# Causal attention: weighting in one block of 512 columns, six slots of probabilities, and 512 columns of zeros added to the sums behind each block

## What is computed

```
xn = layernorm(x)
q, k, v = xn @ Wq.T + bq, xn @ Wk.T + bk, xn @ Wv.T + bv      # 16 heads of 16
p = softmax(q k^T / 4, causal: k_pos <= q_pos)                # per head, 2048 x 2048
s = (p v) @ Wo.T + bo
g = silu(two layers of windowed attention and a gated feed-forward net on xn)
out = x + s * g
```

## Time and profile before

| | us |
|---|---|
| median of 3 runs | 5207.88 |
| lowest, highest | 5165.24, 5208.1 |
| profiled execution | 5235.67 |
| its span | 5233.7 |
| `attend` in it, from the first weighing to the last | 284.6 to 2184.8 |

### The profile page before, as it was taken

The page is one execution under the profiler, slowest core; times in us unless marked ns, Lnnn a source line. Parts: engine busy times, 40 slices in busy tenths (PEclk is TensorE's granted clock), DMA queues, the critical chain, the costliest instruction groups (busy, mean ns, idle before and its releaser), DMA issues. The chain is left out here.

```text
span 5233.7 us, 99917 instructions
## 1 busy us (share of the span) xinstructions
PE 4816.1 (92%) x35808; PEld 3106.5 (59%) x35808; DVE 3696.0 (71%) x7557; ACT 3021.4 (58%) x6873; POOL 1338.9 (26%) x1844
## 2 busy tenths in 40 slices
PE   8599999999999999679999999997699999999986
PEld 7333333343433333267777777775477777777766
DVE  7477776776777777377777777773677777777746
ACT  3156666666666666445666666563366665656642
POOL 3111111111111111143333333330333333333300
PEclk9689888887979798789999999998799999999998
DMA  8623322222222232100000000000100000000007
GB/s 308 180 33 44 48 39 34 35 34 34 35 34 34 34 41 28 65 5 13 14 13 13 13 13 13 13 13 34 33 13 13 13 14 13 17 13 13 13 5 264
DMA packets 175716, 214.72 MB, mean 41 GB/s; under 512 B 75836, under 2 KB 126996, under 8 KB 169108
## 3 DMA queue, kind: packets, MB, share of 16 engines
q1 hardware_dynamic: 175252, 208.56, 17.5%
HBM read 124.05 MB, written 83.89 MB: 40 GB/s over the span
## 5 line engine op out<-in xcount | busy, mean ns | idle before, releaser
L595 ACT ACTIVATE a_pt<-a_ring 128x512 f32<-128x512 f32 (+3 forms) x2560 | 1209.9, 534 | 640.0 <-PE a_ring L678 623.2
L630 DVE TENSOR_REDUCE a_mx<-a_ring 128x2 f32<-128x1024 f32 (+3 forms) x1120 | 1180.2, 1068 | 463.8 <-PE a_ring L691 275.3
L720 PE MATMUL a_ot<-a_pt,a_vt 128*32 128x256 f32 (+2 forms) x8704 | 790.6, 438 | 4.4 <-issue 3.8
L691 PE MATMUL a_ring<-a_ks,a_qs 48*128 48x512 f32 (+3 forms) x2560 | 575.3, 445 | 134.4 <-DMA a_v_in<-v_d 51.4
L678 PE MATMUL a_ring<-a_qs,a_ks 49*128 49x512 f32 (+3 forms) x2560 | 637.6, 497 | 47.9 <-DMA a_qs<-a_ntb 19.2
L970 POOL TENSOR_TENSOR l_rn<-l_ssm,l_half 128x8 f32<-128x8 f32 x256 | 431.8, 1687 | 951.1 <-DVE l_ssm L1252 951.1
L678 PEld LDWEIGHTS a_ring<-a_qs,a_ks 49*128 49x128 f32 x2560 | 263.6, 201 | 558.5 <-issue 196.8
L572 POOL TENSOR_TENSOR a_gate<-a_gate 128x1 f32<-128x1 f32 x512 | 98.8, 193 | 1659.9 <-ACT a_pt L595 1655.1
L1071 ACT ACTIVATE l_pr<-l_pr,l_negm 128x256 f32<-128x256 f32 (+1 forms) x1024 | 500.7, 493 | 6.5 <-DVE l_negm L1304 6.1
L977 POOL TENSOR_TENSOR l_work<-l_work,l_rot 128x512 f32<-128x512 f32 x256 | 357.0, 1396 | 396.2 <-DVE l_work L1260 396.2
L1079 ACT ACTIVATE l_pts<-l_banks 128x512 f32<-128x512 f32 (+1 forms) x512 | 296.9, 580 | 271.7 <-PE l_banks L1581 210.0
(11 more groups left out here) (173 smaller groups left out, 9254.8 us busy)
## 6 DMA issues: line engine op xcount, KB each, us to landing
qk_d<-p_parts SPq DMA_DIRECT2D x16, 2048.0 KB, 10.1
a_qs<-qk_d SPq DMA_DIRECT2D x96, 256.0 KB, 8.9
a_ks<-qk_d SPq DMA_DIRECT2D x96, 256.0 KB, 18.9
x_d<-l_dx SPq DMA_DIRECT2D x32, 512.0 KB, 2.8
l_xt<-x_d SPq DMA_DIRECT2D x24, 513.0 KB, 3.9
p_x_in<-x SPq DMA_DIRECT2D x16, 512.0 KB, 8.6
x_d<-p_xt SPq DMA_DIRECT2D x16, 512.0 KB, 4.8
v_d<-p_vt SPq DMA_DIRECT2D x16, 512.0 KB, 10.4
```

The source lines that it names most:

```text
L595: act.activation(pt[:, s % NPT, j, q0:CHUNK], bank("step", k, f)[:, q0:CHUNK], ACT.Exp).then_inc(exp_done.sem, 1)
L630: r = dve.tensor_reduce(mx[:, pr, :, t, kc], ring[:, a:b + 1, 0:w], AX.X, ALU.max)
L691: mm = pe.matmul(bank("unit", n, f)[:, 0:w], qs[rows, v, pr, q0:q0 + P], ks[rows, v, pr, kc * CHUNK:kc * CHUNK + w], start=True, stop=kc < c)
L720: mm = pe.matmul(ot[j * VW:(j + 1) * VW, a:b], vt[:, v, kt, j], pt[:, s % NPT, j, a:b], start=kt == 0, stop=kt == TPC * (c + 1) - 1)
```

## The change

Each step is weighed as one block, in its second slot, over all its columns (512, on the diagonal 512, 384, 256 and 128), three steps behind instead of two (LAG = 3). `pt` gets six slots. Behind the block of every step but the last of a chunk, four more matmuls follow, one for each head: bfloat16 zeros, 512 columns, added to the same bank, so that the sums stay what they are. The step is counted as weighed (`pv_done`) when these are through. Two tiles of zeros are set by DVE at the start.

```diff
-        NPT = 4
-        LAG = 2
+        NPT = 6
+        LAG = 3
...
+        rest_w = sb("rest_w", [P, VW], BF16)
+        rest_x = sb("rest_x", [P, CHUNK], BF16)
...
+            dve.memset(rest_w[:, :], 0.0)
+            dve.memset(rest_x[:, :], 0.0)
             dve.memset(ones[:, :], 1.0).then_inc(ones_set, 1)
...
                     q0 = first_column(c, kt)
-                    halves = [(max(q0, a), a + CHUNK // 2) for a in (0, CHUNK // 2)]
-                    now = halves[piece:piece + 1] if kt else [(0, CHUNK)] if piece else []
-                    if s == 0 and piece:
+                    if not piece:
+                        return
+                    if s == 0:
                         pe.wait_ge(v_ready.sem, v_ready.at(G))
-                    if kt == 0 and piece:
+                    if kt == 0:
                         pe.wait_ge(os_ready.sem, os_ready.at(G, c))
-                    if now and kt >= TPC * c:
+                    if kt >= TPC * c:
                         pe.wait_ge(masked.sem, masked.at(G, 2 * kt + 2))
-                    elif now:
+                    else:
                         pe.wait_ge(exp_done.sem, exp_done.at(G, GH * (s + 1)))
-                    for a, b in now:
-                        for j in range(GH):
-                            if a < b:
-                                mm = pe.matmul(ot[j * VW:(j + 1) * VW, a:b], vt[:, v, kt, j],
-                                               pt[:, s % NPT, j, a:b],
-                                               start=kt == 0, stop=kt == TPC * (c + 1) - 1)
-                    if piece:
-                        mm.then_inc(pv_done.sem, 1)
+                    for j in range(GH):
+                        mm = pe.matmul(ot[j * VW:(j + 1) * VW, q0:CHUNK], vt[:, v, kt, j],
+                                       pt[:, s % NPT, j, q0:CHUNK],
+                                       start=kt == 0, stop=kt == TPC * (c + 1) - 1)
+                    if kt < TPC * (c + 1) - 1:
+                        for a in range(0, 512, CHUNK):
+                            for j in range(GH):
+                                mm = pe.matmul(ot[j * VW:(j + 1) * VW, 0:min(CHUNK, 512 - a)], rest_w[:, :],
+                                               rest_x[:, 0:min(CHUNK, 512 - a)], start=False, stop=False)
+                    mm.then_inc(pv_done.sem, 1)
```

## The result

The changed kernel takes **5286.42 us** (median of 4 runs, 5279.85 to 5307.62), the kernel before 5196.47 beside it (4 runs, 5165.24 to 5208.1): 1.0174 times as long, 95% interval 1.0137 to 1.0211. The forecast was 5270, slower than before. The profiled execution went from 5235.67 to 5284.91 us, +49 where the sum said +40.

What follows compares the result with a forecast made beforehand. Bound: a 31.5 us DMA chain from load to slot 24, then PE, with low clock costing 7.2 us a period. Terms 2.7 + 5.5 - 5.8 = +2.4 over 14 periods, +6 at the ends: 5276, taken as 5270 us; range 5170 to 5340.

Steps and rivals of the forecast that it cites:

- Part A: From a load's first DMA to slot 24: a chain of DMAs, 31.5 us, not shrunk by the change.
- The later load: Load waits for the last weighing, moved from slot 3 to slot 5: +2.7 us a period (bounds 2.2 to 3.2).
- Block, zeros and wait: Slots 24 to 79 on PE, merged blocks, added zeros and newly exposed waits together: +5.5 us a period (1.0 to 9.5).
- My sign for it: In the changed profile, the zeros row should stand 0.24 us before the following scores.
- dear zeros: Rival: each block of zeros on PE costs 0.355 us, not 0.24, 42 us more in all: 5312 us; chance 0.10.
- The wait itself: Second unit of a full step waits 0.2 to 0.4 us for the first exponential on ACT; step takes 2.91 us.
- The clock: PE's low clock behind slot 24 shrinks to 5 us, its cost from 7.2 to 1.4: -5.8 us a period.
- The sum: All terms of a period: 2.7 + 5.5 - 5.8 = +2.4 us for each of 14 periods, +34.
- The ends: First and last group, outside the periods: zeros and waits cost about 12 us, better clock returns about 6, +6.
- the clock did not pay for all: Denies the rival that zeros keep PE's clock up and the wait vanishes: 5165 us, faster; chance 0.17.
- it did mind: Denies the rival that the clock gains nothing from zeros or new short waits undo them: 5335 us; chance 0.15.
- The three chances: Overall verdict on the changed kernel's time: faster 0.12, same 0.33, slower 0.55.

Runs made afterwards that it cites:

- e14: Kernel before with six slots, three steps of lag and the load at slot 10 instead of 6; halves, no zeros: 5169.65 us, ratio 0.984-0.9959.
- e5: Changed kernel with the load at slot 10 of SP's order instead of slot 6: 5234.96 us, 1.0013-1.0078 of the kernel before.
- e1: Changed kernel without the zeros; one block, six slots and three steps of lag stay: 5224.67 us, 1.000-1.004 of the kernel before.
- e11: Changed kernel without any zeros and with the load at slot 10 instead of 6: 5127.74 us, 0.9811 of the kernel before.
- e13: Kernel before with three steps of lag and six slots of probabilities alone; halves, no zeros: 5214.44 us, ratio 0.9952-1.0017.
- e4: Kernel before with only the load moved from slot 6 to slot 10 of SP's order: 5226.33 us, ratio 0.9952-1.0051.
- e9: Changed kernel with most zeros moved to the end of a step's first slot, ahead of the second unit: 5277.13 us, 1.0085-1.0218 of the kernel before.
- e2: Kernel before with zeros added behind the second half of each step; halves and lag of two stay: 5216.33 us, ratio 0.9965-1.0032.
- e7: Kernel before with zeros behind the second half of each step and the load at slot 10: 5241.43 us, ratio 1.0036-1.0098.

## Why the prediction was right

**Part A** was to stay a chain of DMAs of 31 to 32 us: 30.9, and slot 24 still released by the maxima. But I had PE stand there for 5 us or more, and it stood 44.1 / 14 = 3.2. I had read the kernel before wrongly here. It does not wait at slot 24 "in every period" but in 9 of 14, 19.2 / 14 = 1.4 us in the mean, and the second period of the earlier trace rows is one of the five without: its clock was already low for 20.5 us in slots 5 to 14, PE came later than the maxima, and A took 32.8 us. So low clock inside A is not always free either. The sum lost little by it, since the mean of A moved by 0.6.

**The later load** was +2.7. The load begins 6.6 us behind slot 0, 4.4 before: +2.2, and A, which I had as fixed, gave 0.6 back. Slots 0 to 23 grew by 1.6.

**Block, zeros and wait** were +5.5 (bounds 1.0 and 9.5). At full clock slots 24 to 79 took 32.0 + 43.9 = 75.9 in halves (e14's good group) and 35.7 + 48.2 = 83.9 in e5: +8.0. This is the term that was mis-sized, and it splits in two. The zeros are 83.9 - 78.7 = 5.2 for 26 blocks, 0.20 each, where I had 6.2 at 0.24; the lower bound of 0.215, from the slope of float32 columns, was the nearer. (My sign for it, 0.24 from the zeros row to the next scores, was badly chosen: that distance is 0.33, near the 0.35 that was to speak for dear zeros, because the zeros start 0.88 behind the block and not 1.00. The price is the 1.21 from block to scores less the 1.00.) The Trainium skill's 2.38 times for three packed column tiles (TensorE: Matmul & The Clock Gate, Part 3, measured speedups), which I had scaled to 0.27, is not borne out for four bfloat16 tiles behind a block in the same tiling. The block form alone, e1, is 33.4 + 45.3 = 78.7, +2.8, where my working (the merge gains 0.23 in every merged pair, the wait costs 0.42 in the eight full ones and some 0.2 in six) gives -0.6. The wait itself was forecast and is there, 0.37 in 0.2 to 0.4, but a full step takes 2.98 and not 2.91. The traces of e11 and e14, step by step at full clock (medians of their groups), show the rest: a plain full step takes 2.76 in the block form and 2.48 in halves, +0.28 where I had +0.19; the two steps of 384 columns with a masked unit take 3.60 and 3.52 against 3.18 and 3.10, +0.42, where I had nothing; and of the pairs that were to gain 0.23 each by the merge, five gain 0.14 to 0.33 and seven gain nothing.

**The clock** was -5.8: from 7.2 us of cost to 1.4. Measured in slots 24 to 47, the cost was 40.6 - 32.0 = 8.6 and is 37.9 - 35.7 = 2.2: -6.4. I had taken "no low clock" there as 33 us and it is 32, so both kernels lose more than I said. Low clock behind slot 24 went from 24 us to 5.2, as forecast (5), and the stage's clock to 0.95 (0.93 or more). What brought it down I had only in part. One edit after the other, with the load at slot 6, low clock in slots 24 to 47 was 24.0 us before, 16.6 with the third step of lag (e13), 9.7 with the block too (e1), 5.2 with the zeros too. The lag, which the prediction has down for a later load and nothing else, took off as much as the block, and more than the zeros. The whole program's clock says so as well: 0.914 to 0.927 in ten runs of e13, 0.903 to 0.920 in the 17 of the kernel before beside them. That the term still came out so near is in part luck.

**The sum** was +2.4 a period; 1.6 + 8.0 - 6.4 = +3.2 by these parts, and +3.2 from slot to slot. The ends were to bring +6: 49 - 14 x 3.2 = 4. So the forecast was right for most of its reasons; the block, 2.5 us too cheap, was made up in part by a later load 1.1 and a clock gain 0.6 better than forecast. The medians are 90 us apart and the profiled executions 49, because that of the kernel before lay 39 us above its median and that of the changed kernel 1.5 below; I had taken off 6 us for this, and 5270 is 16 us short. The three rivals with a price of their own are out: the clock did not pay for all, it did mind, and the zeros were not dear. The three chances don't follow from their own parts: those give slower 0.58 x 2/3 + 0.25 = 0.64 and same 0.24, where the prediction has 0.55 and 0.33.

One reason held only in part: that PE's wait at slot 24 is what makes the clock fall. In the kernel before, 8 of the 9 periods with the wait have the clock fall between 1.3 us before and 0.5 us behind the start of slot 24, two more have it behind a stop without releaser in slot 23, and in three it falls 5.7 us behind, with no stop at all. Taking the wait away left 14.9 of 24.0 us (e4), 6.9 of 16.6 (e14 for e13) and none of 9.7 (e11 for e1). And the zeros, which were to bring it back, were not needed: e1 has none and a clock of 0.92, e11 has none and 0.96. The Trainium skill's rule behind one rival (the same page, "A second HAM failure mode: psum-queue depth-cycling": short idle moments between groups of matmuls keep the clock going up and down) is not what happened either: 267 such moments of 0.37 us came in, and the clock rose; in e9 they went away and it fell from 0.96 to 0.94. **Open** stays why halves lose the clock where the block keeps it, at the same arithmetic and with PE busier; why the third step of lag keeps it up; and whether the stops in e4 and e7 are late instructions.

## What to carry to other kernels

Filler work that keeps the clock up must be priced like any other: here 36 blocks of zeros cost 6.9 us a period, and the clock that they held was to be had for less by a change in the order of a DMA queue together with the block form and a third step of lag. Put small transfers that someone waits for ahead of a bulk load, and look again at every filler once the wait that it was made for is gone. When halves are merged to one block, write down what each instruction left standing alone will now wait for: a bank of the same step, here 0.37 us in 267 places.

## What was not expected of the hardware

- Matmuls on zeros count toward the clock. Halves with zeros ran at 0.94, halves without at 0.86, and in the block form 0.96 against 0.92. With the load later they add next to nothing to the block form: 0.97 (e5) against 0.96 (e11).
- Low clock can go on with PE busy almost throughout: 0.56 over 49.3 us with PE busy for 48.52. The window from 400 to 1960 of e2 and of the kernel before has it over the whole stage: 0.94 and 0.86 with PE busy for 1475 and 1463 of 1560 us. First e2:

```profile
400.00:1960.00 1560.00, 1474.87 (x15078) 646.42 (x15078) 1145.63 (x1333) 1021.54 (x2193) 243.57 (x868) 0.94 0.27 37
```

then before:

```profile
400.00:1960.00 1560.00, 1462.64 (x13165) 618.86 (x13163) 1138.92 (x1327) 1021.98 (x2185) 241.78 (x860) 0.86 0.27 37
```

- An output DMA stays 15 to 23 us in issue behind a load of 13 DMAs: 19 to 23 with the load at slot 6 in the kernel before and the changed one, 16 to 20 with it at slot 10 in e11.
- PE stops for up to 6.2 us (e7; 4.9 in the middle of a weighing in e4), 15 to 30 us behind the start of a load, with no releaser in the profile, and nearly only where the weighing is in halves.
- Executions of the kernel before differ among themselves by 1.5% (5204.4 to 5280.5, 17 runs), those of e11 beside them, whose clock stays up, by 0.5% (6 runs).
